# Adding rows to router weight differences by accumulating transfers into SBUF instead of on VectorE, and another order of the work between attention and routing

## What is computed

```python
x = x + xattn(layernorm(x), ctx, Wq, Wkv_expand, Wout)   # 16 heads of 32, causal
x = x + ffn(layernorm(x), router_w, router_b, expert_w, expert_b)

def ffn(h):                                              # h: 4096 tokens x 512
    logits = (h @ router_w.T + router_b).reshape(T, O, E) # 512 outputs x 8 experts
    w, sel = top_k(softmax(logits), 2)                   # per token and output
    w = w / sum(w)
    c = zeros((T, E)).at[t, sel].add(w)                  # summed over the outputs
    return einsum('te,teo->to', c, einsum('th,eoh->teo', h, expert_w) + expert_b)
```

## Time and profile before

| | us |
|---|---|
| median of 3 runs | 1985.57 (1982.93 to 1987.98) |
| the profiled execution | 1985.84 |
| its span, first to last instruction | 1984.1 |
| outside the span | 1.7 |
| TensorE busy | 1911.7 (96%) |
| VectorE busy | 1434.7 (72%) |
| ScalarE busy | 1039.1 (52%) |
| GpSimd busy | 847.2 (43%) |
| mean granted TensorE clock | 0.991 |

### The profile page before, as it was taken

How to read it: one execution, slowest core, us unless ns; L and a number is a source line. 1 busy time by engine, 2 the same in 40 slices (tenths; PEclk the granted TensorE clock), 3 DMA queues, 4 the chain that set the end, 5 groups by cost and what they waited for, 6 DMA issues and landing times.

```text
span 1984.1 us, 30426 instructions
## 1 busy us (share of the span) xinstructions
PE 1911.7 (96%) x9772; PEld 1513.8 (76%) x9772; DVE 1434.7 (72%) x2840; ACT 1039.1 (52%) x2062; POOL 847.2 (43%) x1016
## 2 busy tenths in 40 slices
PE   4899999999998999999999999999999999999999
PEld 3667766777665788888888888788888888888887
DVE  5677667767668658787888888477777777777732
ACT  2566566566554347877777877533443333344400
POOL 4587777777674135455444435102321111232100
PEclk8999999999999999999999999999999999999999
DMA  5454554455466478786756555822232222223111
GB/s 166 116 124 131 141 144 126 125 149 138 104 159 236 159 229 272 227 277 219 251 209 217 183 193 196 305 93 79 94 118 85 80 95 85 80 87 124 49 42 33
DMA packets 103693, 294.54 MB, mean 148 GB/s; under 512 B 13777, under 2 KB 14801, under 8 KB 98482
## 3 DMA queue, kind: packets, MB, share of 16 engines
q1 hardware_dynamic: 91394, 209.44, 32.7%
q10 hardware_dynamic: 8880, 67.37, 10.6%
q0 software_dynamic: 3328, 16.78, 3.6%
HBM read 150.31 MB, written 109.16 MB: 131 GB/s over the span
## 4 chain that ended last, share of the span: by engine, by line
PE 83%; DVE 8%; DMA 3%; ACT 2%; issue 2%; SPq 0%; POOL 0%; ACTq 0%; DVEq 0%; POOLq 0%
PE pair L261 20%; PE pair L263 20%; PE pair L262 20%; PE pair L668 4%; PE ps L717 4%; PE ps L261 3%; PE pair L701 3%; PE ps L262 3%; PE ps L263 3%; DMA w_raw<-w_fix 1%; DMA xb<-x 1%; DVE pair L1388 1%; DVE w_raw L1523 1%; PE ps L737 1%; DVE nmax L1382 1%
## 5 line engine op out<-in xcount | busy, mean ns | idle before, releaser
L261 PE MATMUL pair<-w_h,hT 128*128 128x512 f32 x1920 | 752.0, 392 | 5.4 <-ACT w_h L1199 3.6
L263 PE MATMUL pair<-w_h,hT 128*128 128x512 f32 x1920 | 748.7, 390 | 0.0
L262 PE MATMUL pair<-w_l,hT 128*128 128x512 f32 x1920 | 748.4, 390 | 0.0
L1906 POOL TENSOR_TENSOR logits<-logits,second 128x512 f32<-128x512 f32 x224 | 298.3, 1369 | 590.9 <-DVE second L1603 590.6
L261 PEld LDWEIGHTS pair<-w_h,hT 128*128 128x128 f32 x1920 | 361.1, 188 | 81.2 <-issue 5.0
L263 PEld LDWEIGHTS pair<-w_h,hT 128*128 128x128 f32 x1920 | 361.1, 188 | 75.9
L262 PEld LDWEIGHTS pair<-w_l,hT 128*128 128x128 f32 x1920 | 361.3, 188 | 74.3
L1706 DVE SCALAR_TENSOR_TENSOR xb<-pair,c_all,xb 128x512 f32<-128x512 f32 x256 | 191.8, 749 | 195.5 <-PE pair L263 189.4
L1093 ACT ACTIVATE pT<-pair,zero 128x1024 f32<-128x1024 f32 (+3 forms) x256 | 202.7, 792 | 191.4 <-PE pair L701 183.8
L1388 DVE CUSTOM_DVE_ANT_0 pair<-pair,future 128x256 f32<-128x256 f32 (+3 forms) x340 | 184.2, 554 | 122.3 <-PE pair L668 114.0
L1189 ACT ACTIVATE w<-tree 128x512 f32<-128x512 f32 x32 | 20.3, 635 | 389.4 <-DVE tree L1605 389.3
(11 more groups left out here) (166 smaller groups left out, 2609.9 us busy)
## 6 DMA issues: line engine op xcount, KB each, us to landing
logits<-lg_all ACTq DMA_DIRECT2D x32, 1792.0 KB, 8.8
qk_st<-qk SPq DMA_DIRECT2D x372, 128.0 KB, 2.4
lg_all<-ev_a SPq DMA_DIRECT2D x31, 768.0 KB, 8.5
lg_all<-ev_b SPq DMA_DIRECT2D x31, 768.0 KB, 4.6
xb<-x SPq DMA_DIRECT2D x64, 256.0 KB, 2.9
hT_all<-hT SPq DMA_DIRECT2D x32, 512.0 KB, 4.5
hT<-hT_all SPq DMA_DIRECT2D x32, 512.0 KB, 4.1
xt<-in_x SPq DMA_DIRECT2D x8, 1024.0 KB, 5.3
```

The source lines that it names most:

```text
L261: pe.matmul(dst, lh, rh, start=start, stop=False)
L262: pe.matmul(dst, lh, rl, start=False, stop=False)
L263: return pe.matmul(dst, ll, rh, start=False, stop=stop)
L1906: pool.tensor_tensor(logits[t % 2][:, e - 1, :], logits[t % 2][:, e - 1, :], second[:], ALU.subtract)\
```

## The change

- `fix_router` loses its two pieces that add the row; `FIXES` is 3. It waits on `row{k}_in` in place of `fix{k}_in`.
- GpSimd issues, for every weight k, an accumulating transfer that adds `rows_less[k]`, now 2048 elements wide in memory, to `w_raw[:, k]`, once that weight has landed: weight 0 before step (1, 6) of the last batch, 1 before (2, 0), 2 before (2, 6), weights 3, 4 and 5 before (3, 7), weight 6 after the second `deviation`.
- `rows_e` and `rows_l` hold only the bias rows and are no longer filled by `spread`.
- The token blocks count on one semaphore for each buffer, and `load_block` no longer waits.
- `hi_router(1)` moves from (3, 4) to ScalarE's epilogue; `lo_router(1)` and `lo_router(4)` and `normed(2, 0)` change their places.

```diff
-        rows_less = nc.dram_tensor("rows_less", [ND, O], F32, kind="Internal").ap()
+        rows_less = nc.dram_tensor("rows_less", [ND, KC * O], F32, kind="Internal").ap()
...
-        FIXES = 5
+        FIXES = 3
...
+        ROWS_ADDED = {(1, 6): (0,), (2, 0): (1,), (2, 6): (2,), (3, 7): (3, 4, 5)}
-        HI_EARLY = ((3, 1), (3, 4))
+        HI_EARLY = ((3, 1),)
...
                         sp.wait_ge(s["prep_ok"], 3)
-                        sp.dma_start(rows_less, neg_row[0:ND, :]).then_inc(s["prep_out"], 16)
                         for a in range(KC):
                             cols = slice(a * O, (a + 1) * O)
+                            sp.dma_start(rows_less[:, cols], neg_row[0:ND, :]).then_inc(s["prep_out"], 16)
...
-                sp.dma_start(rows[:, :, 1, :], spread(rows_less[ks, :])).then_inc(done, 16)
-                sp.dma_start(rows[0:1, :, 0, :], rows_bias[ks, :].rearrange("k o -> () k o")).then_inc(done, 16)
+                sp.dma_start(rows[0:1, :, :], rows_bias[ks, :].rearrange("k o -> () k o")).then_inc(done, 16)
...
-            def load_block(t, i, name):
-
-                if some(t * 16):
-                    sp.wait_ge(s[name], t * 16)
-                sp.dma_start(xb[i][:], x1[bass.ds(t * P, P), :]).then_inc(s[name], 16)
+            def load_block(t, i):
+                sp.dma_start(xb[i][:], x1[bass.ds(t * P, P), :]).then_inc(s[f"xb_in{i}"], 16)
...
             def epilogue():
                 hi_outputs(NB - 2, KC - 2, B - 1)
+                hi_router(1)
                 hi_router(2)
...
-                        if at == 9:
+                        if at == 7:
                             normed(2, 0)
...
-                lo_router(1)
                 lo_block(0, 0)
                 for i in range(QB):
                     residual_last(i)
                 lo_block(1, 1)
+                lo_router(1)
                 lo_router(2)
...
                 if q == 0:
-                    dve.wait_ge(s[f"fix{k}_in"], 16)
+                    dve.wait_ge(s[f"row{k}_in"], 16)
...
-                elif q < 4:
-                    dve.wait_ge(s["fw_fix"], k * FIXES + q - 1)
-                    row = rows[:, j, 1:2, :].broadcast_to([P, KC // 2, O])
-                    dve.tensor_tensor(w, w, row, ALU.add).then_inc(s["fw_fix"], 1)
...
+                lo_router(4)
                 whole(5)
-                lo_router(4)
...
-                dve.wait_ge(s["xb_in"], (t + 1) * 16)
+                dve.wait_ge(s[f"xb_in{i}"], (t // 2 + 1) * 16)
...
+            def add_router_row(k):
+
+                pool.wait_ge(s[f"fix{k}_in"], 16)
+                if k == 0:
+                    pool.wait_ge(s["prep_out"], PREPARED)
+                pool.dma_start(w_raw[:, k].rearrange("p c o -> p (c o)"),
+                               rows_less[k:k + 1, :].broadcast_to([P, KC * O]), accum_op=ALU.add,
+                               max_dma_last_dim=8192).then_inc(s[f"row{k}_in"], 16)
...
                     for v in range(UNITS):
+                        if not more:
+                            for k in ROWS_ADDED.get((c, v), ()):
+                                add_router_row(k)
...
             deviation(1, 1, "ln2")
+            add_router_row(ND - 1)
```

More of the change, by code:

```diff
@@ L159, in build @@
         ev_a = ffn("ev_a", [P, 3, O], F32, at=hole_h)
-        rows_e = ffn("rows_e", [P, EARLY, 2, O], F32, at=raw_at + slot * (NE + 2))
+        rows_e = ffn("rows_e", [P, EARLY, O], F32, at=raw_at + slot * (NE + 2))
         base_e = ffn("base_e", [P, KC, O], F32, at=raw_at + slot * (NE + 2) + 8 * EARLY * O)
-        rows_l = ffn("rows_l", [P, ND - EARLY, 2, O], F32, at=raw_at + slot * (NE + 5) - 4 * O)
+        rows_l = ffn("rows_l", [P, ND - EARLY, O], F32, at=raw_at + slot * (NE + ND - 1) - 4 * O)
         base_l = ffn("base_l", [P, KC, O], F32, at=free_at)
@@ L208, in build @@
             logs recips refined o_ok o_hi o_lo wo_mm x1_ok xr_in0 xr_in1 x1_out0 x1_out1
-            fw_hi fw_lo prep_in prep_ok prep_out base_in late_in fw_fix fixed fix_erows one_ok xb_in ln2_st ln2_var ln2_rs ln2_nm ln2_nb hn_ok
+            fw_hi fw_lo prep_in prep_ok prep_out base_in late_in fw_fix fixed fix_erows one_ok xb_in0 xb_in1 ln2_st ln2_var ln2_rs ln2_nm ln2_nb hn_ok
             hT_mm hT_hi hT_lo lg_mm lg_ok lg_out_a lg_out_b lg_out_c lg_in0 lg_in1 top gap_ok th_ok second_ok u_ok w2_ok count first_step c_sum c_half c_ok
@@ L216, in build @@
         names += [f"fix{k}_in" for k in range(ND)]
+        names += [f"row{k}_in" for k in range(ND)]
         s = {n: sem(n) for n in names}
@@ L344, in over_batches @@
             epilogue()
-        PREPARED = 16 * (2 + KC)
+        PREPARED = 16 * (1 + 2 * KC)
         RAW_BASE = routerT[:, 0, :].rearrange("(c p) o -> p c o", p=P)
@@ L351, in raw_router @@
             return routerT[:, k + 1, :].rearrange("(c p) o -> p c o", p=P)
-        def spread(rows):
-            return rows.rearrange("k o -> () k o").broadcast_to([P, rows.shape[0], O])
         def stack_heads(queue, c, pair):
@@ L482, in epilogue @@
                 sp.wait_ge(s["shifted"], NB * UNITS)
-                load_block(0, 0, "xb_in")
-                load_block(1, 1, "xb_in")
+                load_block(0, 0)
+                load_block(1, 1)
                 sp.wait_ge(s["pv"], (NB - 1) * QB + 1)
@@ L538, in router @@
                     sp.wait_ge(s["hT_mm"], t + 1)
-                    load_block(t + 2, i, "xb_in")
+                    load_block(t + 2, i)
                 store_logits(t, "a", 3, ev_a[:], 0, 3)
@@ L547, in first_two @@
                     sp.wait_ge(s["hT_mm"], i + 1)
-                    load_block(i + 2, i, "xb_in")
+                    load_block(i + 2, i)
                 for k in (0, 3):
@@ L1519, in fix_router @@
                     if k == EARLY:
-                        dve.wait_ge(s["late_in"], 3 * 16)
+                        dve.wait_ge(s["late_in"], 2 * 16)
                 rows, base, j = (rows_e, base_e, k) if k < EARLY else (rows_l, base_l, k - EARLY)
@@ L1523, in fix_router @@
                     dve.tensor_tensor(w, w, base[:, half], ALU.subtract).then_inc(s["fw_fix"], 1)
-                elif q < 4:
-                    dve.wait_ge(s["fw_fix"], k * FIXES + q - 1)
-                    row = rows[:, j, 1:2, :].broadcast_to([P, KC // 2, O])
-                    dve.tensor_tensor(w, w, row, ALU.add).then_inc(s["fw_fix"], 1)
-                else:
-                    dve.wait_ge(s["fw_fix"], k * FIXES + 3)
-                    dve.tensor_copy(w_raw[0:1, k, 0, :], rows[0:1, j, 0, :]).then_inc(s["fw_fix"], 1)
+                else:
+                    dve.wait_ge(s["fw_fix"], k * FIXES + 1)
+                    dve.tensor_copy(w_raw[0:1, k, 0, :], rows[0:1, j, :]).then_inc(s["fw_fix"], 1)
             def fix_rest():
```

2 lines of the change are left out of this document (1 added, 1 removed).

## The result

The changed kernel took 1992.4 us (median of 8 runs, 1988.95 to 1993.78), the kernel before 1986.15 on the same chip (8 runs, 1982.93 to 1987.98): ratio 1.0032, 95% interval 1.0023 to 1.004. It is 6.25 us slower; +5.0 was forecast. The profiled execution is one of the longer ones, 1993.78 us with a span of 1992.1, so the two traces differ by 8.0.

What follows compares the result with a forecast made beforehand. TensorE, busy 96% of the span, loses time only where idle or at the lower clock. Routing's later start +12.1 and shorter passage after it -7.1 gave +5.0 on 1985.57: 1990.6 us, range 1973 to 1997.

Steps and rivals of the forecast that it cites:

- After routing begins: Routing's start to the last of 14 products: 38.5 us instead of 45.6, TensorE's 1.65 and 3.02 us stops gone; -7.1.
- cover: Time the row transfers have before they are needed: rows 3 to 6 must land by 6 to 20 us after routing begins.
- The price, 5.2 us of all engines, and the sharing: Each accumulating transfer holds all 16 DMA engines 5.2 us, as into memory; transfers beside it share by packets.
- Rival 2: Adding into SBUF costs the same as loading, 2.7 us per transfer: about -3.8, 1981.8 us; chance 0.14.
- Rows 0 and 1: Residual store issued at 595.6 lands at 611.0, not 602.7: two accumulations more (10.3), `rows_e` less (2.0).
- Group 3 starts 3.6 late: SyncE waits for the residual store, so shift rows go at 611.4 instead of 607.83; group 3 on TensorE 3.6 us late.
- rival 3: Row 2 rides ahead of the shift rows, group 3 starts 3.6 + 5.2 late: +10.2, 1995.8 us; chance 0.26.
- Rows 2, 3, 4: Weight 5 lands at 638.9 behind three accumulations; GpSimd waits, and group 30's low part ends at 641.3 instead of 628.9.
- Block 0: First token block's load, issued 641.7, lands 4.3 us later alone, up to 5.2 more beside row 5; 648.6 taken.
- Sum (+12.1 - 7.1): Block 0's statistics, setting routing's start, 12.1 us later; the stretch after routing begins 7.1 shorter: +5.0 in all.
- Rival 1: The transfers hide, so only VectorE's savings count: -2.9 - 1.7 - 7.1 = -11.7, 1973.9 us; chance 0.24.
- GpSimd's issues, 0: GpSimd's seven transfer issues, 0.87 us each, fall in idle time, time regained or waits already counted: 0.

Runs made afterwards that it cites:

- experiment 5: Changed kernel, rows 3-4, 3-5 or 3-6 by late transfers (3 and 4 once the first two blocks landed), others on VectorE: 1983.09, 1987.98, 1983.23 us.

## Why the prediction held, and which of its steps did not

The forecast named +5.0; medians say +6.25, the traces +8.0. Its range, 1973 to 1997, holds, and so does its leaning (0.39 for no change that can be told, 0.34 for slower). Step by step:

- **After routing begins, -7.1:** measured -6.7 (38.9 us for 38.5). Both stops and the lower clock behind them went, and row 6 was no later than its cover.
- **The price, 5.2 us of all engines, and the sharing:** 5.05 and 5.25 where it can be read for three and four rows. Rival 2 falls with it.
- **Rows 0 and 1:** the store was to land 15.4 us after its issue and took 15.66. Right. The first 1.2 us of group 3's delay lie ahead of all this: the same store was issued at 596.79 for 595.6. It is not the rows' doing: the first row left at 593.12, TensorE had stopped 1.61 us for shift rows at 577.39 already, and the kernel with three rows placed late, which has no early row, issued the same store at 596.77.
- **"Group 3 starts 3.6 late":** it started 8.1 late: 1.2 of drift, 3.8 by the store and 3.1 by the shift rows beside row 2. That last part is rival 3, given 0.26 and 5.2 us; it came about at three fifths of its price.
- **"Rows 2, 3, 4": the step that failed.** Weight 5 was to land at 638.9 behind three accumulations, GpSimd to wait for it, and the low part to end at 641.3. It ended at 636.06 and waited for ScalarE. Two things had moved with group 3, which was 8.1 late. Weight 5's load was issued at 623.16 instead of near 613.9, when row 2 (613.06 + 11.3) was almost done: it landed in 7.3 us, at 630.5. And GpSimd came to (3, 7) only at 629.49, for the low part ahead of it in its stream ended at 629.55 (621.1 before): rows 3 and 4 left as weight 5 landed and did not hold it up. In the kernel with rows 0 and 1 earlier GpSimd was there with weights 4 and 5 still on their way, and the step came about.
- **"Block 0": 4.3 to 9.5 us to land, taken 6.9:** it took 16.58, the term most mis-sized. With no wait for weight 5, rows 3 to 5 left together and 7 us ahead of the block load, and all three came before it. Its issue at 636.62 was 5.1 earlier than forecast; its transfer took 9.7 more than forecast; so it landed at 653.2, 4.6 later.
- **Sum (+12.1 - 7.1):** the statistics moved by +16.7 where +12.1 was forecast, routing's start by +16.2, its length by -6.7: +9.5 at the fourteenth product. Of that 1.6 came back behind it, at two stops of TensorE that the changed kernel lacks (waits of the kernel before from 691 to 1300: in total, times, longest):

```profile
PE ps L900 <- ACT xb L1204: 1.6, 2, 0.9
```

That leaves +7.9, against 8.0 between the spans. So the near agreement of +5.0 with +6.25 is in part luck: the wait for weight 5 was forecast and did not happen (-5.1), the load of block 0 was held far longer than forecast (+9.7), and only the difference shows in the time.
- **Rival 1, the best case -11.7:** the kernel without the rows gives -16.0 (-14.9 at the fourteenth product), so what VectorE could gain before routing was under-priced by some 4 us. Nothing hid the transfers, though, and the rival fell on that.
- **GpSimd's issues, 0:** they cost the changed kernel nothing that its trace shows. Moved ahead of block 0's `deviation` they cost 2.0 us (experiment 5).

## What to carry to other kernels

An operation moved from an engine to an accumulating transfer is not gone. Here 1 MB held all 16 DMA engines for 5 us, and the bill came to whoever had 256 KB or 8 KB on the way at that moment. Before such a move, list each transfer in the window for which an engine or a queue waits, stores included, and add to each one all the accumulations that can be in flight with it; look for the wait that makes several leave together. Ask too what stands behind the issue in the issuing engine's stream: two issues ahead of block 0's `deviation` kept VectorE waiting 2.0 us more. And check the free window against the whole train: with three rows behind the block loads in place of two, VectorE stood 5.40 us for the residual sums' store.

## What was not expected of the hardware

Packets of 2 KB instead of 8 KB for the adding transfers left the total about the same (5.8 us a row for 5.05 to 5.6) and shortened the small store's wait only from 15.7 to 13.8 us. A copy of the same bytes held the engines about half as long as the addition, and yet three copies beside the weights' loads kept a 256 KB store for 17.4 us (10.3 before): over half of the transfers' bill, 12.6 of 22.2 us, is there without any adding.
